# Expert, router and hidden operands as fp16 pairs, with weight slabs scaled by powers of two, in a linear-attention and mixture-of-experts kernel

## The reference

```
x = x + attention(layernorm(x))      # 16 heads of 16: qkv, rope, phi = elu + 1,
                                     # causal linear attention: kv += k v^T, ks += k,
                                     # out = q kv / max(q ks, 1e-6), then @ w_out
n = layernorm(x)
weights = routing(sigmoid(n @ Wr / temperature))        # [tokens, 8 experts]
gate, up = n @ Wg[e], n @ Wu[e]                         # 256 -> 256, for every expert e
x = x + sum_e weights[:, e] * ((silu(gate) * up) @ Wd[e])
```

## Time and profile before

| | us |
|---|---|
| median of 3 runs | 807.97 |
| lowest and highest | 806.35, 808.09 |
| span of the profiled execution | 806.5 |
| TensorE, VectorE busy | 760.2, 603.2 |
| ScalarE, GpSimd busy | 465.4, 484.7 |

### The profile page before, as it was taken

The page is one execution under the profiler, slowest core; times in us unless marked ns, Lnnn a source line. Parts: engine busy times, 40 slices in busy tenths (PEclk is TensorE's granted clock), DMA queues, the critical chain, the costliest instruction groups (busy, mean ns, idle before and its releaser), DMA issues.

```text
span 806.5 us, 18062 instructions
## 1 busy us (share of the span) xinstructions
PE 760.2 (94%) x6660; PEld 654.1 (81%) x6660; DVE 603.2 (75%) x1596; ACT 465.4 (58%) x886; POOL 484.7 (60%) x538
## 2 busy tenths in 40 slices
PE   4475899999999999999999999999999999999997
PEld 2364688888888888888888888888888888888886
DVE  6788797878877797778877797787877787765433
ACT  3664776666566656666666556657665566534221
POOL 3785678765666665655666666566666555653232
PEclk9676799999999999999999999999999999999999
DMA  4544124122211123122101221121111121100000
GB/s 139 127 103 110 41 78 93 40 43 68 40 28 24 34 66 41 41 43 54 41 20 35 43 66 40 41 43 27 41 40 40 41 53 28 27 1 27 1 1 27
DMA packets 97319, 38.27 MB, mean 47 GB/s; under 512 B 74192, under 2 KB 96976, under 8 KB 97232
## 3 DMA queue, kind: packets, MB, share of 16 engines
q1 hardware_dynamic: 90704, 30.83, 18.1%
q10 hardware_dynamic: 6528, 6.29, 2.7%
...
## 4 chain that ended last, share of the span: by engine, by line
PE 88%; DVE 5%; POOL 2%; ACT 2%; issue 1%; DMA 1%; SPq 0%; DVEq 0%; ACTq 0%; POOLq 0%
PE y L446 22%; PE gate L413 22%; PE up L413 21%; PE front L288 5%; PE back L333 3%; PE front L289 3%; PE back L369 2%; PE back L344 2%; PE up L381 1%; PE front L311 1%; PE front L394 1%; PE back L326 1%; PE back L356 1%; POOL a_lo L1131 1%; PE back L311 1%
## 5 line engine op out<-in xcount | busy, mean ns | idle before, releaser
L1159 POOL TENSOR_TENSOR h_lo<-work,h_hi 128x512 fp32r<-128x512 f32 x128 | 166.3, 1299 | 66.0 <-ACT h_hi L640 66.0
L1131 POOL TENSOR_TENSOR a_lo<-am,a_hi 128x512 f16<-128x512 f32 x120 | 144.6, 1206 | 54.9 <-ACT a_hi L568 52.3
L446 PE MATMUL y<-wd_hi,h_hi 128*128 128x256 f32 x512 | 148.1, 289 | 1.7 <-DVE xa L1032 1.7
L446 PE MATMUL y<-wd_lo,h_hi 128*128 128x256 f32 x512 | 143.9, 281 | 0.0
L446 PE MATMUL y<-wd_hi,h_lo 128*128 128x256 f32 x512 | 143.8, 281 | 0.0
L1020 DVE TENSOR_TENSOR work<-work,up 128x512 f32<-128x512 f32 x128 | 87.1, 680 | 72.1 <-PE up L413 71.7
L640 ACT ACTIVATE h_hi<-work 128x512 fp32r<-128x512 f32 x128 | 80.6, 630 | 64.5 <-DVE work L1020 39.4
L1032 DVE SCALAR_TENSOR_TENSOR xa<-y,wo,xa 128x256 f32<-128x256 f32 x256 | 113.5, 470 | 4.5 <-PE y L446 4.5
L446 PEld LDWEIGHTS y<-wd_hi,h_hi 128*128 128x128 f32 x512 | 96.5, 189 | 4.9 <-issue 2.1
L446 PEld LDWEIGHTS y<-wd_lo,h_hi 128*128 128x128 f32 x512 | 96.4, 188 | 3.1
L446 PEld LDWEIGHTS y<-wd_hi,h_lo 128*128 128x128 f32 x512 | 96.4, 188 | 0.0
(11 more groups left out here) (200 smaller groups left out, 1722.2 us busy)
## 6 DMA issues: line engine op xcount, KB each, us to landing
...
qT<-q_st SPq DMA_TRANSPOSE x32, 3.2
```

Source lines behind the costliest of these rows:

```text
L446: m = pe.matmul(Y[t // 2][:, t % 2 * D:(t % 2 + 1) * D], h_p[hi][:, n % 2, t * P:(t + 1) * P], wd_p[wi][:, u // KI, u % KI, :], start=(n % ...
L1131: pool.tensor_tensor(a_p[1][:, heads(r), :], am_place(g, r).rearrange("p (h n) -> p h n", h=4), a_p[0][:, heads(r), :], ALU.subtract).then ...
L1159: pool.tensor_tensor(h_p[1][:, n % 2, :], hb[:, n % 2, :], h_p[0][:, n % 2, :].bitcast(F32), ALU.subtract).then_inc(s_hlo, 1)
```

## The change

The parts of expert and router weights, of `x2` and of `h` become fp16. So that weights keep within fp16's range, each slab is multiplied by a power of two that is found on the chip from its norm, and the factors are taken out again further on.

- **Loading.** All 24 slabs have a place of their own (`raw`). SyncE's queue loads them: three after the small inputs, then five in each step s behind the transposes, ahead of the other loads of the step.
- **Norm.** ScalarE squares each slab with a sum per row (`squares(n)`, 24 of them, and `wr_squares`; all stand in the head's order). In five batches (router and slabs 0 to 2, slabs 3 to 5, 6 to 8, 9 to 11, 12 to 23) TensorE sums over the rows with a matrix of ones (`totals`), VectorE takes the sum out of PSUM (`totals_kept`), GpSimd raises it to -1/2 (`inv_norm`), VectorE keeps the exponent bits (`scale`).
- **Parts.** `slab_hi` is a copy with the scale read per partition, `slab_lo` a VectorE scalar_tensor_tensor (raw x scale - high) for all slabs. In the loop, slabs 12 to 23 are prepared in steps 6, 7 and 8.
- **Taking it out.** `silu` gets 1/scale as its scale, `h_up` becomes a scalar_tensor_tensor with a factor per expert, the router's `wo` is multiplied once more by a factor per expert, and the router's temperature takes the scale of Wr (`unscale`, `rtemp_half`).

```diff
+W_TOP = 2.0 ** 14
+H_TOP = 2.0 ** -21
+EXPONENT = 0x7F800000
...
-        wr_s = sb("wr_s", [P, KD, 2, E], F32R)
-        wg_p = [sb(f"wg_{s}", [P, E, KD, I], F32R) for s in ("hi", "lo")]
+        wr_s = sb("wr_s", [P, KD, 2, E], F16)
+        wg_p = [sb(f"wg_{s}", [P, E, KD, I], F16) for s in ("hi", "lo")]
...
+        raw = sb("raw", [P, SLABS, KD, I])
+        ones = sb("ones_m", [P, P])
...
-        x2 = [sb(f"x2_{s}", [P, 2, KD, B], F32R) for s in ("hi", "lo")]
+        x2 = [sb(f"x2_{s}", [P, 2, KD, B], F16) for s in ("hi", "lo")]
...
-        h_p = [sb(f"h_{s}", [P, 2, B], F32R) for s in ("hi", "lo")]
+        h_p = [sb(f"h_{s}", [P, 2, B], F16) for s in ("hi", "lo")]
...
-            n = HEAD_SLABS + STEP_SLABS * (s - LAG) + i
-            return n if i < STEP_SLABS and n < SLABS else None
+            n = HEAD_SLABS + STEP_SLABS * (s - LAG - 1) + i
+            return n if s > LAG and i < STEP_SLABS and n < SLABS else None
...
+            def totals(i):
+
+                cols = batch_cols(i)
+                w.wait_ge(s_onem, 1)
+                w.wait_ge(s_sq, cols.stop)
...
+                pe.matmul(total_bank(i)[:, cols], ones[:, :], ssq[:, cols], start=True, stop=True).then_inc(s_tot, 1)
...
+            def squares(n):
+
+                _, dst, e_ = slabs[n]
+                w.wait_ge(slab_in[n // 3], 48)
+                act.activation(dst[1][:, e_, :, :], raw[:, n, :, :], ACT.Square,
+                               accum_out=ssq[:, 1 + n:2 + n]).then_inc(s_sq, 1)
...
-                act.activation(dst[0][:, e_, :, :], ring[n % NSL], ACT.Copy).then_inc(s_slab_hi, 1)
-                load_slab(n + NSL - 1)
+                act.activation(dst[0][:, e_, :, :], raw[:, n, :, :], ACT.Copy, scale=slab_scale(n)).then_inc(s_slab_hi, 1)
...
-                act.activation(hb[:, n % 2, :], G[:, :], ACT.Silu).then_inc(s_g, 1)
+                act.activation(hb[:, n % 2, :], G[:, :], ACT.Silu, scale=isc[:, 1 + 3 * e_:2 + 3 * e_]).then_inc(s_g, 1)
...
-                v.tensor_tensor(dst[1][:, e_, :, :], ring[n % NSL], dst[0][:, e_, :, :].bitcast(F32),
-                                ALU.subtract).then_inc(s_slab_lov, 1)
+                v.scalar_tensor_tensor(out=dst[1][:, e_, :, :], in0=raw[:, n, :, :], scalar=slab_scale(n),
+                                       in1=dst[0][:, e_, :, :], op0=ALU.mult, op1=ALU.subtract).then_inc(s_slab_lov, 1)
...
-                v.tensor_tensor(hb[:, n % 2, :], hb[:, n % 2, :], U[:, :], ALU.mult).then_inc(s_h, 1)
+                v.scalar_tensor_tensor(out=hb[:, n % 2, :], in0=U[:, :], scalar=ch[:, e_:e_ + 1], in1=hb[:, n % 2, :],
+                                       op0=ALU.mult, op1=ALU.mult).then_inc(s_h, 1)
```

The orders of the head, of TensorE, ScalarE, VectorE and SyncE, where the new calls stand:

```diff
+            qkv(0); qkv(1); totals(0); scores(0, 0); scores(0, 1); qkv(2); av(0); state(0); scores(1, 0); o_T(0)
+            totals(1); scores(1, 1); qkv(3); proj(0); av(1); scores(2, 0); state(1); x2_T(0); totals(2); scores(2, 1)
+            o_T(1); qkv(4); proj(1); av(2); state(2); x2_T(1); scores(3, 0); o_T(2); totals(3); scores(3, 1); proj(2)
...
+            x_hi(1); wout_hi(); wr_squares(); squares(0); squares(1); squares(2); qk_copy(0); v_copy(0); v1(0)
...
+            q_hi(1); k_hi(1); slab_hi(2); x_hi(3); squares(3); a_hi(0, 0); a_hi(0, 1); a_hi(0, 2); a_hi(0, 3)
...
+            v_copy(3); squares(7); a_hi(2, 0); slab_hi(4); s1(1); exp(3); a_hi(2, 1); v1(3); squares(8); x2_hi(0)
...
+            x2_hi(2); slab_hi(8); squares(13); o_hi(3); squares(14); squares(15); s1(3); s2(3); v2(4); slab_hi(9)
+            squares(16); slab_hi(10); squares(17); squares(18); slab_hi(11); a_hi(4, 0); squares(19); x2_hi(3)
+            a_hi(4, 1); squares(20); squares(21); squares(22); squares(23)
...
+            den_rec(3); norm(3); x_lo(5); slab_lo(6); slab_lo(7); slab_lo(8); x2_lo(2); scale(3); o_lo(3); st_add(3); x1_add(3)
...
                 load_xr(s + 2)
                 transpose_q(s); transpose_k(s)
+                for n in range(5 * s + 3, 5 * s + 8):
+                    load_slab(n)
```

More of the change, by code:

```diff
@@ L11 @@
 BF16 = mybir.dt.bfloat16
+I32 = mybir.dt.int32
 ALU = mybir.AluOpType
@@ L473, in wr_hi @@
                 w.wait_ge(c_wr, 16)
-                act.activation(wr_s[:, :, 0, :], wr_sb[:, :, :], ACT.Copy).then_inc(s_wr_hi, 1)
+                w.wait_ge(s_sc, 1)
+                act.activation(wr_s[:, :, 0, :], wr_sb[:, :, :], ACT.Copy, scale=sc[:, 0:1]).then_inc(s_wr_hi, 1)
             def wqkv_hi(k):
@@ L648, in scalar_program @@
[L648 to L652 removed]
+            x_hi(0); wqkv_hi(0); wqkv_hi(1)
@@ new lines, in scalar_program @@
+            x_hi(1); wout_hi(); wr_squares(); squares(0); squares(1); squares(2); qk_copy(0); v_copy(0); v1(0)
+            exp(0); k_hi(0); q_hi(0); qk_copy(1); v2(0); slab_hi(0); x_hi(2); v_copy(1); v1(1); exp(1); slab_hi(1)
+            q_hi(1); k_hi(1); slab_hi(2); x_hi(3); squares(3); a_hi(0, 0); a_hi(0, 1); a_hi(0, 2); a_hi(0, 3)
+            squares(4); v2(1); qk_copy(2); squares(5); x_hi(4); v_copy(2); v1(2); exp(2); a_hi(1, 0); v2(2); k_hi(2)
+            s1(0); q_hi(2); o_hi(0); a_hi(1, 1); squares(6); s2(0); a_hi(1, 2); a_hi(1, 3); qk_copy(3); slab_hi(3)
@@ new lines, in scalar_program @@
+            v_copy(3); squares(7); a_hi(2, 0); slab_hi(4); s1(1); exp(3); a_hi(2, 1); v1(3); squares(8); x2_hi(0)
+            q_hi(3); k_hi(3); a_hi(2, 2); o_hi(1); a_hi(2, 3); wr_hi(); slab_hi(5); s2(1); qk_copy(4); x_hi(5)
+            v2(3); squares(9); s1(2); v_copy(4); x2_hi(1); squares(10); a_hi(3, 0); o_hi(2); a_hi(3, 1); squares(11)
+            exp(4); s2(2); a_hi(3, 2); a_hi(3, 3); q_hi(4); k_hi(4); slab_hi(6); v1(4); slab_hi(7); squares(12)
+            x2_hi(2); slab_hi(8); squares(13); o_hi(3); squares(14); squares(15); s1(3); s2(3); v2(4); slab_hi(9)
@@ L1052, in vector_program @@
-            mean_var2(2); var_eps2(2); k_lo(4); q_lo(4); o_sum(3, 0); o_sum(3, 1); ln2(2); den_max(3); den_rec(3)
-            norm(3); x_lo(5); x2_lo(2); o_lo(3); st_add(3); x1_add(3); bn2(3); mean_var2(3); var_eps2(3); mask(4, 0)
-            ln2(3); mask(4, 1); var_eps(5); x2_lo(3); slab_lo(11)
+            tcos_scale(0); wout_lo(); x_lo(1); cos(0); rope(0); phi(0); totals_kept(0); tcos_scale(1); q_lo(0); cos(1)
+            scale(0); k_lo(0); rope(1); x_lo(2); phi(1); tcos_scale(2); q_lo(1); mask(0, 0); mask(0, 1); k_lo(1)
@@ new lines, in vector_program @@
+            mask(0, 2); slab_lo(0); mask(0, 3); slab_lo(1); cos(2); o_sum(0, 0); bn(4); o_sum(0, 1); rope(2); den_max(0)
+            tcos_scale(3); den_rec(0); mask(1, 0); phi(2); norm(0); st_add(0); mask(1, 1); x_lo(3); q_lo(2); slab_lo(2)
+            totals_kept(1); mask(1, 2); k_lo(2); mean_var(4); var_eps(4); mask(1, 3); o_lo(0); cos(3); x1_add(0); bn2(0)
+            mean_var2(0); o_sum(1, 0); var_eps2(0); o_sum(1, 1); scale(1); bn(5); mask(2, 0); st_add(1); den_max(1)
+            ln2(0); rope(3); mask(2, 1); den_rec(1); mean_var(5); norm(1); x_lo(4); phi(3); x2_lo(0); totals_kept(2)
@@ new lines, in vector_program @@
+            mask(2, 2); slab_lo(3); mask(2, 3); q_lo(3); tcos_scale(4); o_lo(1); k_lo(3); cos(4); x1_add(1); bn2(1); mean_var2(1); var_eps2(1)
+            o_sum(2, 0); o_sum(2, 1); ln2(1); den_max(2); slab_lo(4); den_rec(2); st_add(2); wr_lo()
+            norm(2); scale(2); mask(3, 0); mask(3, 1); slab_lo(5); x2_lo(1); rope(4); o_lo(2); totals_kept(3); mask(3, 2); mask(3, 3); phi(4)
+            x1_add(2); bn2(2); mean_var2(2); var_eps2(2); k_lo(4); q_lo(4); o_sum(3, 0); o_sum(3, 1); ln2(2); den_max(3)
@@ L1239, in sync_program @@
             load_small()
+            for n in range(3):
+                load_slab(n)
             for s in range(STEPS):
```

197 lines of the change are left out of this document (122 added, 75 removed).

## The result

The changed kernel takes 815.4 us (median of 4 runs, 813.5 to 816.8), beside 808.0 for the kernel before (806.4 to 808.5): a ratio of 1.0094, 95% interval 1.0073 to 1.0114. The forecast was 795 us. The time lies 2.4 us above the range, on the side that had a chance of 0.19. The profiled execution has a span of 812.8 us.

A forecast was written before the change was run, and what follows sets the result against it. TensorE bounds the steady stretch; VectorE and GpSimd are busiest between 40 and 60 us. Span 806.5 - 34 - 4.5 + 10 + 3 + 2.8 + 10 = 793.8, so 795 us measured; range 778 to 813.

The forecast's parts named there:

- Part 4: Head: squares, low parts and load order delay the first gate matmul from 83.7 to 94 us; 10 us more (3 to 22).
- Part 1: Expert matmuls on TensorE: fp16 operands save 13.5 and 8.5 ns each, 34 us, plus 4.5 us at late weights.
- Part 2: Steady steps: waits at proj and up(n+3) lose 0.35 us of TensorE's gain per step, 10 us in all.
- Part 3: Main loop's weight preparation: 3 us for low parts, 2.8 us for one wait in step 8, nothing for router scaling and second unscale.
- The hole at up(14): Step 8: up(14) waits once for slab 22's low part on VectorE, 2.8 us (0 to 4).
- The order of the loads: Head: SyncE's five slab loads ahead of xr(3) make x_hi(3) wait until 31.5 us; 3 us.
- The low parts on VectorE: Head: three low parts stand ahead of x2_lo(2), which proj(3) needs; 1.4 us.
- Squares with totals: Head: totals(2) and totals(3) wait for squares, 1.5 and 1.2 us; six more ScalarE instructions ahead of x2_hi(3), 2.4 us.
- Rival 3: Head: scale round trips over five engines stall it; first gate at 114, later than about 107 decides; 815 us; chance 0.12.
- Rival 1: Steady steps: TensorE's 38.5 us gain arrives whole, no loss at meeting points, head 4 us; 776 or 779 us; chance 0.16.
- Rivals 2 and 4: Expert matmuls no faster in 16 bits, 819 us, chance 0.08; side engines' chain sets the step, 814 us, chance 0.05.
- Rival 5: Head: ScalarE's Square needs its own table, 16 loads of 1.28 us, half on the path; 805 us; chance 0.04.

The follow-up runs named there:

- fp16_only: The kernel before with the router's and experts' weights, x2 and h as two fp16 parts, no scaling, loads and low-part split as before: 779.7 us.
- slab_early: The changed kernel with the third slab of steps 5 to 8 prepared right behind the second on ScalarE and VectorE: 810.6 us.
- wo_late: The changed kernel with the multiplication of the router's weights by the y factors moved behind the step's last h product on VectorE: 808.3 us.
- xr_first: The changed kernel with SyncE's loads of x, transposed x and table issued ahead of each step's five slab loads: 810.6 us.
- squares_xr: The changed kernel with x loads ahead of slab loads, ScalarE's squares kept, no totals, pow, scales or unscales, factors set to 1.0: 803.2 us.

## Why the prediction was wrong, by its own steps

**What bounds the kernel.** Right for the steady stretch; in the head GpSimd (17.89 of 20 us) was busier than VectorE, which Part 4 calls the busiest. But VectorE's 4.9 free microseconds are a mean over unequal steps. In the kernel before VectorE is busy for 17.1 of 22.7 us in a plain step and for 20.7 of 22.7 in a router step. That step, with the least room, was never costed.

**Part 1** was right: 109 and 216 ns, against the 109.5 and 215.5 taken. The Trainium skill (TensorE: Matmul & The Clock Gate, "Back-to-back issue gap") gives the formula that leads to 109 and 216 ns for one isolated warm matmul, and for a stream with a weight load before each matmul 131 ns at 512 columns. The prediction leaves that condition out. This stream, with a weight load each, ran at 216 ns: the measurement agrees with the first figure and not with the second. fp16_only gives the sum of parts 1 and 2 as 28.3 us; they had 38.5 - 10 = 28.5.

**Part 2** was right, in size and mainly in place. A plain step came to 21.75 us in fp16_only, 0.95 less than before, where the instructions alone should give 1.2. The missing 0.25 are at the projection, a wait for VectorE. TensorE's own rows in fp16_only show no wait there, its weight load (PEld) does:

```profile
319.80 0.59 PE L413 MATMUL gate<-x_lo,wg_hi 128*128 128x512 f16 x2
319.94 0.41 DVE L860 TENSOR_TENSOR ox_lo<-back,ox_hi 128x256 fp32r<-128x256 f32 x1
320.40 0.30 PEld L369 LDWEIGHTS back<-wout_hi,ox_hi 128*128 128x128 f32 x2 [0.50 <-DVE ox_lo L860]
320.40 0.50 PE L369 MATMUL back<-wout_hi,ox_hi 128*128 128x256 f32 x2
320.74 0.39 PE L369 MATMUL back<-wout_lo,ox_hi 128*128 128x256 f32 x2
...
321.21 0.60 PE L413 MATMUL up<-x_hi,wu_hi 128*128 128x512 f16 x2
```

In the kernel before that weight was loaded ahead of the projection at 330.91:

```profile
330.69 0.42 PEld L369 LDWEIGHTS back<-wout_hi,ox_hi 128*128 128x128 f32 x2
```

Two gate matmuls of 216 ns from 319.80 on would let the projection start at 320.23. It starts at 320.40, 0.05 us behind the end of `ox_lo` (320.35), and its first pair takes 0.34 us, where with its weight loaded ahead it took 0.24 (330.91 to 331.15): 0.17 and 0.10, together some 0.27 us a step. The prediction had 0.15 to 0.2 for this wait. At `up(n + 3)` the trace has a small one as well (weight loads wait for `x_lo` in seven of nine steps between 300 and 500 us, up to 0.2 us). That the total of 10 us fits so well is partly luck: the router steps lose 0.4 us more than the plain ones, which no term had.

**Part 3** had three terms. The 3 us for the low parts were more than enough: against fp16_only steps 6 and 7 are 1.0 us longer in the change, and step 8 without its hole (slab_early) 0.5. The hole at up(14) was right in place and size (2.9 us for 2.8; it came 90 us behind the first gate, not 75), but not in price: with the slow clock behind it step 8 cost 4.3 us more, shown by slab_early. "Router scaling (8 small instructions) and the second unscale lie in VectorE's free time and are on nobody's way: nothing" is the step that failed: 6 us in the router steps, shown by wo_late, which only moves that one instruction. It stands in the chain ahead of the h product that TensorE waits for, in a step without room, and it takes 1.08 us where 0.19 would do, because it is held up until a GpSimd instruction ends. The second unscale, with the totals, pow and scales of the fifth batch that stand in the same step, cost step 5 about 2.9 us (26.6 in xr_first, 23.6 in squares_xr); their shares are not parted.

**Part 4** named the mechanisms of the head, but summed 10 us where it was 17.7 against fp16_only. Three terms were too small. The order of the loads: 3 us taken, 5.1 measured; of the two waits for x only the first was followed, and not the load of x itself. The low parts on VectorE: 1.4 taken for three of them, 3.6 to 4.3 measured. Their own length was not the error, ten of the head's twelve take 0.74 us in the change and the prediction had 0.86; only one place was costed. Which of the other places cost the rest no run shows. Squares with totals: 2.4 + 1.5 + 1.2 taken, 4.6 + 4.4 measured. The first gate came at 100.8, not at 94.

**The sum** in its own terms: parts 1 and 2 -28.5 (measured -29.4 in spans), head +10 (+17.7 against fp16_only), part 3 +5.8 (+18.0 for everything behind the head against fp16_only). Of the 19.0 us by which the span missed the sum, 7.7 are the head's and 12.2 the loop's, less 0.9 in parts 1 and 2: the larger part is not in the head, which got a rival of its own, but in the loop, most of it in the place of the router's multiplication (6.0) and in step 5 (4.2 over fp16_only).

**The rivals.** Rival 3 gave 815 us, which is the time measured, but not for its reason: the first gate came before its 107 us, so the match is luck. Rival 1 fell: fp16_only, with all side work gone, keeps 28.3 of the 38.5 us that it counts on, and waits at the projection. That its 779 is near fp16_only's 779.7 is luck as well, since it holds 9.8 us of side work that fp16_only does not have. Rivals 2 and 4 fell with the stream and the plain steps. Rival 5 fell too: between the table load at 0.80 us and that of the first silu at 103.17 there is none, with all 25 squares between them.
